# Causal heads of 64: the second pair of scores of a group is issued directly behind the first

## The reference

```python
h = _rms(x, ln_w)
q = (h @ wq).reshape(B, S, NHEADS, HEAD_DIM)      # 32 heads of 64
k = (h @ wk).reshape(B, S, KVHEADS, HEAD_DIM)     # 8 key heads
v = (h @ wv).reshape(B, S, KVHEADS, HEAD_DIM)
q, k = _rope(q, k)
k = jnp.repeat(k, g, axis=2)                      # g = 4
v = jnp.repeat(v, g, axis=2)
scores = jnp.einsum('bqhd,bkhd->bhqk', q, k) / np.float32(np.sqrt(HEAD_DIM))
scores = jnp.where(causal[None, None], scores, jnp.float32(-1e+30))
attn = jax.nn.softmax(scores, -1)
o = jnp.einsum('bhqk,bkhd->bqhd', attn, v).reshape(B, S, NHEADS * HEAD_DIM)
x = x + o @ wo
```

## Time and profile before

| | |
|---|---|
| median of 3 runs | 3724.21 us (3715.98 to 3729.96) |
| span of the profiled execution | 3687.3 us |
| TensorE matmuls busy | 3303.7 us |
| VectorE busy | 2631.0 us |
| ScalarE busy | 1933.5 us |
| GpSimd busy | 990.3 us |
| granted TensorE clock, 300 to 400 us | 1.00 |

### The profile page before, as it was taken

The page is one execution under the profiler, slowest core; times in us unless marked ns, Lnnn a source line. Parts: engine busy times, 40 slices in busy tenths (PEclk is TensorE's granted clock), DMA queues, the critical chain, the costliest instruction groups (busy, mean ns, idle before and its releaser), DMA issues. The chain is left out here.

```text
span 3687.3 us, 65201 instructions
## 1 busy us (share of the span) xinstructions
PE 3303.7 (90%) x22154; PEld 2194.8 (60%) x22154; DVE 2631.0 (71%) x8703; ACT 1933.5 (52%) x5275; POOL 990.3 (27%) x960
## 2 busy tenths in 40 slices
PE   6999999987997899997899999988799749999975
PEld 4666767664554344445667667665455437887853
DVE  5888888885444788873788888887344567777755
ACT  4667767664222366774676767666222125555531
POOL 3211112233454001012121212143444332222213
PEclk8999999998998689997999999998899769999986
DMA  4140500013755322302060500011756300000010
GB/s 129 52 170 7 166 1 1 20 48 110 178 91 116 70 46 58 73 23 72 1 220 1 172 1 1 4 48 57 215 88 122 89 1 15 1 16 4 1 34 23
DMA packets 202239, 234.78 MB, mean 64 GB/s; under 512 B 20662, under 2 KB 188536, under 8 KB 201080
## 3 DMA queue, kind: packets, MB, share of 16 engines
q1 hardware_dynamic: 170968, 190.48, 17.0%
q0 software_dynamic: 30944, 40.14, 6.5%
HBM read 98.13 MB, written 133.73 MB: 63 GB/s over the span
## 5 line engine op out<-in xcount | busy, mean ns | idle before, releaser
L1816 ACT ACTIVATE p_prob<-bank,p_small 128x256 f32<-128x256 f32 (+3 forms) x1280 | 646.2, 515 | 156.0 <-DVE p_small L1988 151.3
L1988 DVE CUSTOM_DVE_ANT_0 bank<-bank,p_mask 128x256 f32<-128x256 f32 (+3 forms) x1280 | 579.0, 490 | 97.1 <-PE bank L1559 85.7
L2336 POOL TENSOR_TENSOR p_tm<-p_rope_a,p_rope_b 128x512 f32<-128x512 f32 x192 | 245.8, 1280 | 1269.0 <-DVE p_rope_b L1968 1264.5
L1559 PE MATMUL bank<-p_k,p_q 64*128 64x256 f32 (+3 forms) x3840 | 529.2, 347 | 13.6 <-ACT p_prob L1816 12.5
L1821 ACT ACTIVATE p_prT<-bank 128x512 f32<-128x512 f32 x752 | 426.0, 601 | 211.5 <-PE bank L1568 209.6
L1568 PE MATMUL bank<-g_ident,p_prob 128*128 128x128 f32 x3008 | 438.3, 284 | 54.4 <-DVE p_prob L1997 20.8
L1997 DVE TENSOR_SCALAR p_prob<-p_prob,p_small 128x256 f32<-128x256 f32 (+3 forms) x1280 | 424.5, 395 | 11.3
L1577 PE MATMUL bank<-p_prT,p_v 128*64 128x512 f32 (+1 forms) x1504 | 428.2, 619 | 0.3 <-ACT p_prT L1821 0.3
L1568 PEld LDWEIGHTS bank<-g_ident,p_prob 128*128 128x128 f32 x3008 | 330.0, 142 | 150.6 <-issue 50.2
L1559 PEld LDWEIGHTS bank<-p_k,p_q 64*128 64x128 f32 (+1 forms) x3840 | 339.1, 188 | 116.1 <-issue 65.1
L2034 DVE TENSOR_REDUCE p_nmax<-bank 128x1 f32<-128x512 f32 x512 | 320.8, 683 | 56.8 <-PE bank L1618 54.6
(11 more groups left out here) (288 smaller groups left out, 6215.8 us busy)
## 6 DMA issues: line engine op xcount, KB each, us to landing
sorted<-p_blank SPq DMA_DIRECT2D x32, 2304.0 KB, 19.2
p_w<-in_L_ffn_w SPq DMA_DIRECT2D x96, 256.0 KB, 4.5
p_h_in<-sorted SPq DMA_DIRECT2D x158, 144.0 KB, 2.7
p_k_st<-k_saved SPq DMA_DIRECT2D x16, 288.0 KB
p_q_st<-q_saved SPq DMA_DIRECT2D x16, 288.0 KB
g_stage<-in_L_ffn_wq SPq DMA_DIRECT2D x8, 512.0 KB, 3.8
g_stage<-in_L_ffn_wo SPq DMA_DIRECT2D x16, 256.0 KB, 4.3
q_saved<-p_qp SPq DMA_DIRECT2D x16, 256.0 KB, 3.2
```

The source lines that it names most:

```text
L1559: ins = pe.matmul(h.use.ap[:, 0:n], q[rows, at, :], k[rows, kp, o.g, keys], start=i == 0, stop=i == 2)
L1816: act.activation(s.prob.ap[:, 0:s.o.w], s.use.ap[:, 0:s.o.w], ACT.Exp, bias=sm[:, 0, j:j + 1], scale=-1.0, accum_out=sm[:, 1, j:j + 1]).th ...
L1988: dve.tensor_tensor_reduce(x, x, A.mask[:, A.mask.shape[1] - o.w:], -1.0, FAR, ALU.add, ALU.min, o.sm.ap[:, 0, h.j:h.j + 1]).then_inc(made)
```

## The change

The step `scores` is split in two. `scores` now only has TensorE's matmuls; the new step `row_maxima` has VectorE's maxima and takes the heads that `scores` returns. For causal heads both pairs of a group are scored at its beginning, one directly behind the other, and the maxima of heads 2 and 3 stay where the second pair stood. For wide heads `row_maxima` follows each `scores` at once.

```diff
--- before.py
+++ after.py
@@ -483,13 +483,20 @@
             s.o, s.heads, s.ready = o, [], [o.u.q_made[o.t], o.u.k_made[max(1, o.t)]]
             for j in heads:
                 h = Phase()
-                h.o, h.j, h.use, h.prob, h.max_made = o, j, sring.take(), prob.take(), self.vector_made.up()
+                h.o, h.j, h.use, h.prob = o, j, sring.take(), prob.take()
                 s.heads.append(h)
                 o.probs.append(h.prob)
                 o.scored = h.use.full
+            return s.heads
+
+        waiting = []
+
+        def row_maxima(heads):
+            s = self.step("row_maxima", A)
+            s.heads = heads
+            for h in heads:
+                h.max_made = self.vector_made.up()
                 waiting.append(h)
-
-        waiting = []
 
         def exponentials():
             for sc in waiting:
@@ -596,7 +603,8 @@
                     next(normed[b + 2])
                 cur = group(c, b, unit, t, g)
                 nturn = prev.nkt if prev else 0
-                scores(cur, *((0,) if wide else (0, 1)))
+                pairs = [scores(cur, 0)] if wide else [scores(cur, 0, 1), scores(cur, 2, 3)]
+                row_maxima(pairs[0])
                 weighed = weigh(full) if full else None
                 if prev:
                     normalise(prev)
@@ -606,20 +614,20 @@
                 if weighed:
                     weighed = low_parts(weighed)
                 if wide:
-                    scores(cur, 1)
+                    row_maxima(scores(cur, 1))
                 if settled:
                     project_out(settled)
                     settled = None
                 route_last()
                 beside()
                 if not wide:
-                    scores(cur, 2, 3)
+                    row_maxima(pairs[1])
                 route_last()
                 for kt in range(0, min(2, nturn)):
                     turn(prev, kt)
                 exponentials()
                 if wide:
-                    scores(cur, 2)
+                    row_maxima(scores(cur, 2))
                 beside()
                 if wide and weighed:
                     project_out(weighed)
@@ -629,7 +637,7 @@
                 route_last()
                 exponentials()
                 if wide:
-                    scores(cur, 3)
+                    row_maxima(scores(cur, 3))
                     exponentials()
                 beside()
                 settled = weighed
@@ -1979,10 +1987,10 @@
                                      A.scale, s.k.ap[:, 0, 0:A.nk, tok].bitcast(F32),
                                      ALU.mult, ALU.subtract).then_inc(s.use.free[0].sem)
 
-        elif s.kind == "scores":
-            o = s.o
+        elif s.kind == "row_maxima":
             w.wait_ge(A.masked)
             for h in s.heads:
+                o = h.o
                 x = h.use.ap[:, 0:o.w]
                 w.wait_ge(h.use.full, o.sm.after)
                 dve.tensor_tensor_reduce(x, x, A.mask[:, A.mask.shape[1] - o.w:], -1.0, FAR, ALU.add, ALU.min,
```

## The result

The changed kernel takes 3941.86 us (median of 4 runs, 3934.39 to 3950.71) where the kernel before takes 3727.09 (4 runs). The ratio is 1.0577, 95% interval 1.0551 to 1.0603: slower, inside the stated range, 43 us under the stated 3985.

A forecast was written before the change was run, and what follows sets the result against it. The prediction took TensorE to bound the causal stretch, VectorE close behind. 30 units x 8.45 = 253 us plus 8 us for the last units gave +261; 3687.3 + 261 + 36.9 = 3985 us, range 3915 to 4070.

The forecast's parts named there:

- The mechanism: Causal groups: TensorE's second pair waits until exponentials of heads 2 and 3 free their banks; 6.2 + 0.4 us a unit.
- The weighing held back in (t3,g1): In (t3,g1) the second pair goes ahead of the weighing and holds it back by its own length, 0.89 us.
- The rotation in (t0,g0): In (t0,g0) the second turned tile waits for the bank VectorE's rotation frees; exponentials end 0.55 us later.
- The k turns: Other three groups with a k turn: turns follow it 0.55 us sooner; cost between 0 and 1.65 us, taken as 0.4.
- What comes back: Two score blocks in a row could save a fixed 0.21 us each; taken as 0, up to 1.7 us a unit.
- The sum of a unit: A causal unit grows by 6.2 + 0.4 + 0.9 + 0.55 + 0.4 = 8.45 us, from 49.25 to 57.7.
- The router units: Units with router steps: TensorE already waits elsewhere, but the same group pattern holds; no extra term, 8.45 us each.
- rival (a): TensorE's clock falls too in the causal units, adding 45 to 110 us: 4030 to 4095 us; chance 0.14.
- The 36.9 us around the span: Difference between median 3724.21 and profiled span 3687.3, taken to lie around or between runs, untouched by the change.
- (b): Wait absorbed in part: exponentials come earlier as maxima 2 and 3 no longer wait for scores; 3855 us, chance 0.10.
- (c): Faster: banks always free before TensorE needs them, 256 x 0.21 = 54 us saved; 3670 us, chance 0.03.
- (d): Order doesn't change what runs when: TensorE already waits there or goes around the blocked pair; 3724 us, chance 0.03.

The follow-up runs named there:

- experiment 1: Kernel before, scores unmoved, plus a TensorE wait behind each causal group's first pair for the previous group's exponentials 2 and 3 ("wait alone"): 3906.68 us, ratio 1.0479.
- control pair: Kernel before and changed kernel, both unchanged, run once more on one chip: changed kernel 3915.00 us, ratio 1.0624; kernel before 3687.69 us.
- experiment 6: Kernel before, but in (t0,g1), (t1,g0) and (t1,g1) both score pairs, all maxima and all exponentials come at the beginning: 3665.99 us, ratio 0.9964.
- experiment 4: Changed kernel with maxima 2 and 3 directly behind maxima 0 and 1 and all four exponentials together: 3909.12 us, ratio 1.0475.
- experiment 7: Changed kernel's order only in units 0 to 12 of each causal stage, order of before in 13 to 15: 3875.81 us, ratio 1.0522.

## Why the prediction was right

- **The mechanism** held in each part: the wait for banks 2 and 3, in seven groups and not in (t0,g1), paid each time, with a release of 0.05 us. Waits and release were put at 6.2 + 0.4 = 6.6 us in a unit; experiment 1 measured 55.48 - 49.25 = 6.23.
- **The weighing held back in (t3,g1)**, put at 0.9: after less wait alone is 9.23 - 8.34 = 0.89.
- **The rotation in (t0,g0)**, put at 0.55: 7.52 - 6.97 = 0.55.
- **The k turns**, put at 0.4 between 0 and 1.65: (t1,g0) and (t3,g0) have 0.21 and 0.22.
- **What comes back**, taken at 0, bound 1.7, was mis-sized: four groups, (t0,g1), (t1,g1), (t2,g0) and (t2,g1), are 0.13 to 0.15 us shorter than with the wait alone, 0.56 us in all. There the block of scores no longer lies between products or a turn of k and the turns of the probabilities. The rule of the Trainium skill (TensorEngine Tiling (Array Packing), Key Properties) that a change of tiling mode drains TensorE fits this, and the 0.19 us of two blocks in a row; neither run separates the drain from other costs at the start of a block.
- **The sum of a unit**: 8.45 us was said and 7.54 measured, so the 26 units 0 to 12 of the two stages grew by 192.4 us where the sum has 219.7.
- **The router units** are the step that failed. They grew by 12.7 and 15.6 us in the first stage and by 12.5 and 16.9 in the second, where the sum has 8.45 each, and took back 24 us. Their term was "left" with the argument that the same pattern of groups holds. It doesn't: the waits for the banks reach 2.9 and 3.9 us there, and TensorE's clock falls, as rival (a) had it, though not in the stretch that it was stated for. The last units grew by 5.9 and 5.8 us instead of 4.2.
- **The sum over the span**, +261, met +254.6 by errors that cancel, and in part by luck: of the two executions that were compared, that of the kernel before was some 37 us shorter than its group's median and that of the changed kernel was not. The medians of that group differ by 214.8 us, those of the control pair by 227.3. So the forecast is 15 to 22% above what the change costs between runs of one group.
- **The 36.9 us around the span** were the largest error of the forecast. I took the difference between the profiled span and the median for something fixed. It is not: in every run on record the span is only 1.7 to 1.8 us under the time. Without this term the sum is 3948 us, 6 us from the measured 3942; but it then starts from an execution that is some 37 us shorter than the runs it is compared with.
- Rivals (b), (c) and (d) fell. (c) needed E in time in all groups; experiment 6 shows its saving, 0.5 us in a unit, where that is made true in three groups.

## What to carry to other kernels

Before work is issued earlier in an ordered queue, look up when its buffer comes free, and subtract: the difference is a stall for all that stands behind it, and it is paid each time round unless the buffer's release moves too. Check which queues the release hangs on; with two of them, moving one gives little. Moving a step early pays only where the release has already happened, so choose by group, not by loop.

## What the runs showed of the hardware

Two blocks of six 64-row score matmuls at 256 keys take 0.91 us in a row and 1.10 apart. A release from ScalarE to TensorE took 51 to 54 ns in 506 of 508 waits. VectorE's normalising instructions took 0.48 us each, and 3.70 and 2.56 us where they ran beside GpSimd's splitting of weights (experiment 4). In the middle units TensorE kept a granted clock of 1.00 with waits of 0.45 to 1.4 us for the banks, busy for 85.23 of 100 us. In the two router units of experiment 7 it had 0.92 and 0.90 as a mean, and fell to 1.2 GHz, mostly behind waits of 2.2 to 3.9 us, busy for 57.84 of 74.0 and 59.27 of 76.6 us.

The same kernel had medians of 3727, 3684 and 3688 us in groups of runs on different chips, a spread of 1.2%, while the one that waits more had 3942 and 3915. Chip and moment weren't separated. So a ratio of two kernels from one group need not be that of another: 1.058 and 1.062 here, with intervals that just touch.
